# First attention of a vision tower on one Trainium2 core: tokens turned ahead of the last output product, value roots, query sums and the tile table in other places

## The chip, the cores and the metric

The kernel runs on one core of a Trainium2 chip (trn2). The metric is the device time in microseconds (us) of one execution, from inputs in the chip's memory to outputs there. The core's engines are TensorE (PE, matrix products into the PSUM banks; its weight loads are listed as PEld), VectorE (DVE), ScalarE (ACT), GpSimd (POOL) and the queue SP, which only issues transfers here. Each engine works through its own list of instructions in order, and waits on semaphores for the others.

## The reference, cut to what matters

There are 32 samples of 256 tokens with 256 features. Every sample passes a token mixer, then a first attention with 16 heads of 16 key and 64 value features, then a second attention and a layer of 8 experts.

```python
# token mixer
q, k, v = proj(Wq), proj(Wk), proj(Wv)
y = sigmoid(q) * (exp(wb) @ (exp(k) * v)) / (exp(wb) @ exp(k))
h = layer_norm(y @ out_w + out_b + x)           # then a class token is put in front
# first attention, on layer_norm(h)
q, k, v = (l2norm(q), l2norm(k), l2norm(v))
attn = square(relu(einsum('bhid,bhjd->bhij', q, k)))
out = tanh_norm(einsum('bhij,bhjd->bhid', attn, v))
h = h + out @ Wout
# second part: latent attention, then the two best of 8 experts for each token
```

`tanh_norm(t)` is `tanh(n) * t / n` with n the length of t.

## The kernel before, in words

The stages follow each other, each in a block of its own with a barrier of all engines behind it: constants, `mixer_and_attention` (to about 1820 us of the profiled execution), class tokens, `latent_attention` (to about 3029 us), `load_experts`, `plan`, `experts`, `merge`.

`mixer_and_attention` is a software pipeline written out by hand. A loop runs over samples, and in one turn, `sample(i, d, before, more)`, every engine does three things in an order fixed in the code: the products of sample i (eight pairs of heads, p = 0 to 7), the mixer and the projections of the next sample j = i + 1, and the output norm and output product of the sample before, i - 1. Thirty-one turns carry a next sample.

TensorE, for each pair of heads: `sim` (L1105, keys by queries), `attend` (L1115 and L1120, squared weights by values) and `square_sums` (L1127, sums of squares of the outputs, products with only 2 columns). In between stand, for the next sample, the queries and keys of the mixer (`mixer_inputs`, L983 to L989), `mix` (L996), the residual and mixer output, `turn_tokens` (L1031, the transposes of the normed tokens), `project` (L1038), `project_values` (L1062 to L1067), `class_products` (L1075 sums of squares of the keys with 8 columns, L1083, L1087 with 16 columns) and `query_sums` (L1075 again, sums of squares of the queries); and for the sample before `spread_scale` (L1148) and `project_outputs` (L1155, four of them, m = 0 to 3).

What hands over to what, where the change touches it:

- `project_outputs(i-1, 0)` waits for the first scaled outputs OT, which DVE makes (`scale_outputs`, L863). DVE does `first_stats` ahead of it, which in the kernel before ends with two products (L757) that only `first_norm` reads.
- `project_keys` waits for xT, which ACT copies (L613) from the bank that `turn_tokens` fills.
- `attend(i, d, 7)` writes a bank whose sums DVE must have taken (`keep_sums`, L825), and `square_sums(i, 5)` stands directly ahead of it.
- `attend(i, d, 0)` waits for the values V, which POOL scales (`value_rows`, L572). The reciprocal lengths of the values come from a power on POOL (`power`, L66, tile vrn). POOL's order in one turn is: output roots, norm roots, a copy of h1, `class_parts` (L553 to L561), then for each half t of the tokens power, L570 and L572.
- `sim(i, 0)` waits for keys and queries that SP has put through memory (L493 and L502).

`load_experts` loads 16 pieces of expert weights in turns of 4 buffers (SP L2275), splits each into a high part (ACT L2286) and a low part (DVE L2308), makes a few tables on POOL, and at its end writes 16 blocks of zeros into the buffer of routed tokens xg (SP L2279). `plan` then computes on DVE, from the fill of each expert's region, which expert and which row each of 144 tiles has (L2342 to L2369), while SP clears 8 more blocks of xg (L2337).

Of the kernel before, what the change touches and what calls it, by code (L numbers as in the profile page):

```python
# [10 lines left out]
F32 = mybir.dt.float32  # L11
# [360 lines left out]
def mixer_and_attention(nc, v, a, nb):  # L372
# [4 lines left out]
    with ExitStack() as ctx:  # L377
# [158 lines left out]
        @block.gpsimd  # L536
        def _(pool):
            def norm_roots(j):
                pool.wait_ge(ln_stats, 5 * j + 5)
                power(pool, rstd[:, 1], rstd[:, 0], v.inv_root).then_inc(ln_rooted, 1)  # L540
                pool.wait_ge(ln2_stats, 5 * j + 5)
                power(pool, rstd2[:, 1], rstd2[:, 0], v.inv_root).then_inc(ln2_rooted, 1)

            def keep_h1(i, d):
                need(pool, h2_done, i)
                pool.wait_ge(h1_done, LT * i + LT)
                pool.sem_inc(pool_step, 1)
# [17 lines left out]
            def value_rows(j, e, t):  # L565
                pool.wait_ge(v_lift, 2 * j + t + 1)
                power(pool, vrn[:, t], vsm[:, t], v.inv_root).then_inc(v_rn, 1)
                pool.wait_ge(v_rn, 2 * j + t + 1)
                pool.wait_ge(k_inv, j + 1)
                pool.tensor_tensor(vc[:, t], vrn[:, t], rk[:, t], ALU.mult).then_inc(v_c, 1)  # L570
                pool.wait_ge(v_c, 2 * j + t + 1)
                pool.tensor_tensor(V[:, e, t].rearrange("p (g d) -> p g d", d=DV),  # L572
                                   Vr[:, t].rearrange("p (g d) -> p g d", d=DV),
                                   vc[:, t].unsqueeze(2).to_broadcast([P, HEADS, DV]), ALU.mult).then_inc(v_ready, 1)

            def front(j, e):
                norm_roots(j)
                class_parts(j, e)
                value_rows(j, e, 0)
                value_rows(j, e, 1)  # L580
# [130 lines left out]
        def _(dve):  # L711
# [41 lines left out]
            def first_stats(j):  # L753
                dve.wait_ge(hpre_done, j + 1)
                layer_norm_stats(j, mixed, stats, mv, rstd, ln_stats)
                for t in range(LT):
                    dve.scalar_tensor_tensor(ln[:, t], mixed[t], mv[:, t, 0:1], v.g_ln[:], ALU.subtract,  # L757
                                             ALU.mult).then_inc(ln_done, 1)
# [113 lines left out]
            def front(j, e):  # L872
# [5 lines left out]
                first_stats(j)  # L878
                tokens(j + 1)
# [14 lines left out]
            def sample(i, d, before, more):  # L894
# [24 lines left out]
                if before:  # L919
                    scale_outputs(i - 1, 1 - d, 0)  # L920
                    scale_outputs(i - 1, 1 - d, 1)
# [55 lines left out]
        def _(pe):  # L977
            def mixer_inputs(j):
# [5 lines left out]
                last.then_inc(q_done, 1)  # L984
                for t in range(LT):
# [174 lines left out]
            def front(j):  # L1160
                mixer_inputs(j)
# [14 lines left out]
            def sample(i, d, before, more):  # L1176
                j = i + 1
                sim(i, 0)
                if before:
                    square_sums(i - 1, 7)  # L1180
                if more:
                    mixer_inputs(j)
# [23 lines left out]
                square_sums(i, 2)  # L1206
                if before:
# [1045 lines left out]
def load_experts(nc, v, a):  # L2253

    with ExitStack() as ctx:
        NST = 4
# [3 lines left out]
        hi_done, lo_done, idle_clear, misc = sems(nc, ctx, "w_hi", "w_lo", "idle_clear", "d_misc")  # L2260
        block = ctx.enter_context(nc.Block())
        parts = [(v.w1h, v.w1l, e) for e in range(NEXP)] + [(v.w2h, v.w2l, e) for e in range(NEXP)]

        @block.sync
        def _(sp):
# [10 lines left out]
            sp.wait_ge(misc, 6)  # L2276
# [3 lines left out]
            sp.wait_ge(idle_clear, 16 * (v.idle_rows // P))  # L2280

# [7 lines left out]
        def _(pool):  # L2289
            pool.memset(v.zeros[:], 0.0).then_inc(misc, 1)  # L2290
            pool.iota(last_no[:], pattern=[[0, 1]], base=v.out_rows - P, channel_multiplier=1).then_inc(misc, 1)
            for e in range(NEXP):
# [7 lines left out]
                               pattern=[[1, NEXP], [-1, NEXP]], channel_multiplier=0)  # L2300
# [4 lines left out]
        def _(dve):  # L2305
            for n, (h, l, e) in enumerate(parts):
                dve.wait_ge(hi_done, n + 1)
                dve.tensor_tensor(l[:, e], stage[:, n % NST], h[:, e].bitcast(F32), ALU.subtract).then_inc(lo_done, 1)  # L2308


def plan(nc, v):

    with ExitStack() as ctx:
        n_tab = v.tile_no.shape[1]
        n = sbuf(nc, ctx, "p_n", [1, NEXP])
        up = sbuf(nc, ctx, "p_up", [1, NEXP], I32)
        tiles_i = sbuf(nc, ctx, "p_tiles_i", [1, NEXP], I32)
        tiles = sbuf(nc, ctx, "p_tiles", [1, NEXP])
        sums = sbuf(nc, ctx, "p_sums", [1, NEXP, NEXP])
        ends = sbuf(nc, ctx, "p_ends", [1, NEXP])  # L2320
        skip = sbuf(nc, ctx, "p_skip", [1, NEXP])
        tail = sbuf(nc, ctx, "p_tail", [1, NEXP], I32)
        b = sbuf(nc, ctx, "p_b", [1, n_tab])
        past = sbuf(nc, ctx, "p_past", [1, n_tab, NEXP])
        moved = sbuf(nc, ctx, "p_moved", [1, n_tab, NEXP])
        e = sbuf(nc, ctx, "p_e", [1, n_tab])
        row = sbuf(nc, ctx, "p_row", [1, n_tab])
        step, tails, cleared = sems(nc, ctx, "p_step", "p_tails", "p_cleared")
        block = ctx.enter_context(nc.Block())
        fill = v.fill[0:1, v.last_fill]  # L2330

        @block.sync
        def _(sp):
            sp.wait_ge(tails, 1)
            for ex in range(NEXP):
                r = sp.value_load(tail[0:1, ex:ex + 1], min_val=ex * v.rows_e, max_val=(ex + 1) * v.rows_e - P)
                sp.dma_start(v.xg[bass.ds(r, P)], v.zeros[:]).then_inc(cleared, 16)  # L2337
            sp.wait_ge(cleared, 16 * NEXP)

        @block.vector  # L2340
        def _(dve):
            dve.tensor_copy(tail[:], fill).then_inc(tails, 1)  # L2342
            dve.tensor_tensor(n[:], fill, v.region[0:1, :], ALU.subtract).then_inc(step, 1)
            dve.tensor_copy(b[:], v.tile_no[:]).then_inc(step, 1)
            dve.wait_ge(step, 1)
            dve.tensor_scalar(up[:], n[:], float(P - 1), None, ALU.add).then_inc(step, 1)
# [4 lines left out]
            dve.wait_ge(step, 5)  # L2351
            dve.tensor_tensor(sums[:], tiles[:].unsqueeze(1).to_broadcast([1, NEXP, NEXP]), v.upto[0:1],
# [10 lines left out]
            dve.tensor_reduce(e[:], past[:], AX.X, ALU.add).then_inc(step, 1)  # L2363
# [3 lines left out]
            dve.tensor_scalar(v.tile_e[:], e[:], float(NEXP - 1), None, ALU.min).then_inc(step, 1)  # L2367
# [298 lines left out]
def build(nc, a, out):  # L2666
# [14 lines left out]
    with ExitStack() as ctx:  # L2681
# [12 lines left out]
        plan(nc, v)  # L2694
# [73 lines left out]
```

## Time and profile before

| | |
|---|---|
| median of three runs | 3639.7 us (3630.85 to 3646.9) |
| the profiled execution's own time | 3646.67 us |
| its span, first to last instruction | 3643.9 us |
| granted TensorE clock, mean over the span | 0.929 |
| busy share of the span | PE 89%, DVE 58%, ACT 39%, POOL 32% |

The table is read as follows: TensorE is far ahead of the others, and its clock, which has two levels, 2.4 GHz (1.00) and 1.2 GHz (0.50), is at the upper one most of the time. The span leaves 2.8 us of the profiled time outside.

### The profile page before, as it was taken

Reading aid. Unit: us, or ns where it says so; the run is one execution under the profiler, and the core shown is the slowest. Engines: PE = TensorE matmul, PEld = TensorE weight load, DVE = VectorE, ACT = ScalarE, POOL = GpSimd, SP = SyncE. Lnnn points to the kernel's source line nnn. Section 1 sums busy time; section 2 is a strip of 40 time slices with the busy share of each in tenths; the row PEclk is TensorE's granted clock in tenths of the full one; section 3 lists DMA queues with packets and bytes.
Section 4 is the critical chain, followed back from the end, with each engine's and each line's share of the span. In section 5 each row is a group of like instructions: output and inputs, shape, how many; then the busy total and the mean of one; then the engine's idle time right before and its main releaser. Section 6 shows DMA issues by size and latency. Waiting matters only on the chain. (4 is left out here: it accounts for less than half of the span.)

```text
span 3643.9 us, 69402 instructions
## 1 busy us (share of the span) xinstructions
PE 3239.7 (89%) x23216; PEld 2461.1 (68%) x23217; DVE 2117.5 (58%) x5311; ACT 1405.0 (39%) x2820; POOL 1151.8 (32%) x1030
## 2 busy tenths in 40 slices
PE   4899999999999999999977999999999971999990
PEld 2677777777777777777645767777777751999990
DVE  4566656666566666566524666666666653444442
ACT  1443443443443443443412444444444432444440
POOL 2332433423424424424311222222222221444440
PEclk7899999999999999999968999999999995999995
DMA  2232322323323323323300111111111114444449
GB/s 73 76 83 56 78 78 52 86 66 63 86 60 70 86 61 68 86 61 69 81 8 27 34 37 42 44 44 39 36 41 44 41 36 148 77 76 77 76 77 291
DMA packets 219177, 249.00 MB, mean 68 GB/s; under 512 B 36129, under 2 KB 180834, under 8 KB 219122
## 3 DMA queue, kind: packets, MB, share of 16 engines
q1 hardware_dynamic: 184658, 204.82, 21.3%
q0 software_dynamic: 25936, 34.95, 5.8%
q10 hardware_dynamic: 8528, 8.52, 0.7%
q8 instruction: 32, 0.52, 0.1%
q14 instruction: 23, 0.19, 0.0%
HBM read 142.30 MB, written 105.87 MB: 68 GB/s over the span
## 5 line engine op out<-in xcount | busy, mean ns | idle before, releaser
L644 ACT ACTIVATE R<-psA 128x1024 f32<-128x1024 f32 x256 | 262.5, 1025 | 478.3 <-PE psA L1105 476.6
L821 DVE TENSOR_TENSOR PR<-R 128x1024 f32<-128x1024 f32 x256 | 313.6, 1225 | 0.0
L1120 PE MATMUL psA<-PR,V 128*64 128x258 f32 x2048 | 284.1, 398 | 0.0
L1820 DVE TENSOR_REDUCE m_nm<-psC 128x4 f32<-128x516 f32 (+1 forms) x256 | 239.0, 955 | 69.9 <-PE psC L2092 69.3
L1155 PE MATMUL psA<-wout,OT 128*128 128x256 f32 x1024 | 261.5, 400 | 15.5 <-DVE OT L863 15.5
L1691 ACT ACTIVATE m_PT<-psC 128x770 f32<-128x770 f32 x256 | 197.9, 800 | 185.0 <-PE psC L2121 185.0
L1155 PEld LDWEIGHTS psA<-wout,OT 128*128 128x128 f32 x1024 | 188.7, 194 | 48.7 <-DVE OT L863 18.4
L1608 POOL DMA_INDIRECT xg<-r_tn,r_idx x130 | 127.8, 983 | 279.5 <-DMA xg<-r_tn,r_idx 241.2
L1127 PEld LDWEIGHTS psA<-half,osq 128*128 128x128 f32 x1024 | 142.3, 201 | 94.0 <-issue 90.8
L66 POOL TENSOR_TENSOR rstd<-rstd,inv_root 128x2 f32<-128x2 f32 x64 | 45.6, 713 | 469.8 <-DVE rstd L721 469.8
L66 POOL TENSOR_TENSOR vrn<-vsm,inv_root 128x16 f32<-128x16 f32 x64 | 185.2, 2894 | 6.0 <-POOL pcl L561 5.0
L825 DVE COPY ssb<-psA 128x4 f32<-128x4 f32 x256 | 40.6, 159 | 244.9 <-PE psA L1127 243.7
L1120 PEld LDWEIGHTS psA<-PR,V 128*64 128x64 f32 x2048 | 125.8, 138 | 83.4 <-issue 25.9
L66 POOL TENSOR_TENSOR orr<-osm,inv_root 128x32 f32<-128x32 f32 x32 | 174.2, 5443 | 14.7 <-DVE osm L835 14.1
L1680 ACT ACTIVATE m_oa<-psC 128x256 f32<-128x256 f32 x128 | 49.2, 384 | 322.2 <-PE psC L2139 322.2
L649 ACT ACTIVATE oTs<-psA 128x258 f32<-128x258 f32 x256 | 99.0, 387 | 188.8 <-PE psA L1120 184.7
L2422 POOL DMA_INDIRECT out_rows<-e_y,e_dest x69 | 106.8, 1548 | 192.2 <-DVE e_y L2483 189.0
L1127 PE MATMUL psA<-half,osq 128*128 128x2 f32 x1024 | 164.3, 265 | 0.2 <-ACT osq L651 0.2
L2451 ACT ACTIVATE e_sh<-psE 128x512 fp32r<-128x512 f32 x137 | 82.1, 599 | 165.7 <-PE psE L2525 165.7
L2422 POOL DMA_INDIRECT xs<-e_y,e_dest x68 | 105.4, 1550 | 126.4 <-DVE e_y L2483 120.6
L553 POOL TENSOR_TENSOR psq<-prl 80x256 f32<-80x256 f32 x32 | 19.5, 611 | 396.3 <-ACT prl L624 396.3
L1038 PE MATMUL psA<-xT,wqk 128*128 128x256 f32 x512 | 124.8, 399 | 22.0 <-ACT xT L613 22.0
(410 smaller groups left out, 8265.8 us busy)
## 6 DMA issues: line engine op xcount, KB each, us to landing
ks<-parts SPq DMA_DIRECT2D x512, 64.0 KB, 2.2
qs<-parts SPq DMA_DIRECT2D x512, 64.0 KB, 2.3
e_x<-xg SPq DMA_DIRECT2D x143, 129.0 KB
xraw<-in_x SPq DMA_DIRECT2D x66, 256.0 KB
xs<-m_zrow SPq DMA_DIRECT2D x32, 264.0 KB
f_even<-out_rows SPq DMA_DIRECT2D x13, 640.0 KB
f_odd<-xs SPq DMA_DIRECT2D x13, 640.0 KB
out_rows<-f_even ACTq DMA_DIRECT2D x13, 640.0 KB, 5.6
```

Of the source, the lines that this page charges most:

```text
L66: return pool.tensor_tensor(out, x, e.to_broadcast(list(out.shape)), ALU.pow)
L644: act.activation(R[:, p % 2], ps[:, 0:2, :].rearrange("p a (t n) -> p a t n", t=LT), ACT.Relu).then_inc(relu_done, 1)
L649: act.activation(oTs[:, d, p], ps[:, 2 + p % 2, 0:QCOLS], ACT.Copy).then_inc(o_copied, 1)
L821: dve.tensor_tensor(PR[:, p % 2, :, :, 0:L], R[:, p % 2], R[:, p % 2], ALU.mult).then_inc(prob_done, 1)
L1038: last = pe.matmul(ps[:, bank, c * L:(c + 1) * L], v.wqk[:, k, first + c * P:first + (c + 1) * P], xT[:, k, :], start=k == 0, stop=k == KT ...
L1120: last = pe.matmul(ps[64 * hh:64 * hh + 64, 2 + p % 2, 0:QCOLS], V[:, d, t, n * DV:(n + 1) * DV], PR[:, p % 2, hh, t, :], start=False, sto ...
L1127: last = pe.matmul(ps[:, 2 + p % 2, SUMS + 2 * t:SUMS + 2 * t + 2], osq[:, p % 2, t * P:(t + 1) * P], v.half2[:], start=True, stop=True, s ...
L1155: last = pe.matmul(ps[:, BOUT, t * MODEL:(t + 1) * MODEL], OT[:, m % 2, p % 2, t * P:(t + 1) * P], v.wout[:, p, :], start=p == 0 and t == ...
L1608: pool.indirect_dma_start(v.xg, bass.IndirectOffsetOnAxis(ap=idx[rows, d, s, t:t + 1], axis=0), tn[rows, d, s, t], None).then_inc(rows_out ...
L1691: act.activation(PT[:, g % 2, 2 * b:2 * b + 2, :], ps[:, 2 * b:2 * b + 2, 0:3 * P + 1], ACT.Exp).then_inc(exp_done, 1)
L1820: dve.tensor_reduce(nm[:, t, :, DK], ps[:, 0:4, cols], AX.X, ALU.max, negate=True).then_inc(max_done, 1)
L2422: pool.indirect_dma_start(v.odd if b % 2 else out, bass.IndirectOffsetOnAxis(ap=dest[:, b % XD:b % XD + 1], axis=0), y[:, b % XD], None, c ...
```

## The change

On TensorE, within a turn: `mixer_inputs` is cut into `mixer_queries` and `mixer_keys`, and the queries' products stand ahead of `square_sums(i-1, 7)`. `sim(i, 5)` stands ahead of the output products 0 to 2 and the spreads between them. `turn_tokens` stands ahead of output product 3. `query_sums` stands between `square_sums(i, 5)` and `attend(i, d, 7)`, two groups earlier. On DVE: the two products of `first_stats` become `first_scaled` and stand behind `scale_outputs(.., 0)`, and `query_norms` stands ahead of `keep_sums(i, d, 6)`. On POOL: the powers for the values become `value_roots`, and the one for t = 0 stands ahead of `class_parts`. The work of `plan` moves into the block of `load_experts`: on DVE ahead of all low parts, its clears on SP behind the fourth of the 16 weight loads; the wait for the tables is a semaphore instead of the barrier. The block `plan` is gone.

```diff
# POOL
+            def value_roots(j, t):
                 pool.wait_ge(v_lift, 2 * j + t + 1)
                 power(pool, vrn[:, t], vsm[:, t], v.inv_root).then_inc(v_rn, 1)
+
+            def value_rows(j, e, t):
                 pool.wait_ge(v_rn, 2 * j + t + 1)
...
                 keep_h1(i, d)
                 if more:
+                    value_roots(i + 1, 0)
                     class_parts(i + 1, 1 - d)
                     value_rows(i + 1, 1 - d, 0)
+                    value_roots(i + 1, 1)
                     value_rows(i + 1, 1 - d, 1)
# DVE, sample
                     first_stats(j)
                 if before:
                     scale_outputs(i - 1, 1 - d, 0)
+                if more:
+                    first_scaled(j)
+                if before:
                     scale_outputs(i - 1, 1 - d, 1)
...
                     value_lift(j, 1)
+                    query_norms(j, e)
                 keep_sums(i, d, 6)
-                if more:
-                    query_norms(j, e)
# TensorE, sample
                 sim(i, 0)
+                if more:
+                    mixer_queries(j)
                 if before:
                     square_sums(i - 1, 7)
                 if more:
-                    mixer_inputs(j)
+                    mixer_keys(j)
...
                 square_sums(i, 2)
+                sim(i, 5)
                 if before:
                     project_outputs(i - 1, 0)
                     spread_scale(i - 1, 2, more)
                     project_outputs(i - 1, 1)
                     spread_scale(i - 1, 3, more)
                     project_outputs(i - 1, 2)
-                sim(i, 5)
                 attend(i, d, 4)
                 square_sums(i, 3)
+                if more:
+                    turn_tokens(j)
                 if before:
                     project_outputs(i - 1, 3)
                 if more:
-                    turn_tokens(j)
                     project_keys(j)
...
                 square_sums(i, 5)
+                if more:
+                    query_sums(j)
                 attend(i, d, 7)
                 square_sums(i, 6)
-                if more:
-                    query_sums(j)
# load_experts, SP
                 sp.dma_start(dst, src).then_inc(w_loaded[n % NST], 16)
-            sp.wait_ge(misc, 6)
+                if n == NST - 1:
+                    sp.wait_ge(misc, 6)
+                    sp.wait_ge(tails, 1)
+                    for ex in range(NEXP):
+                        r = sp.value_load(tail[0:1, ex:ex + 1], min_val=ex * v.rows_e, max_val=(ex + 1) * v.rows_e - P)
+                        sp.dma_start(v.xg[bass.ds(r, P)], v.zeros[:]).then_inc(cleared, 16)
...
             sp.wait_ge(idle_clear, 16 * (v.idle_rows // P))
+            sp.wait_ge(cleared, 16 * NEXP)
# load_experts, DVE: the instructions of plan (L2342 to L2369), then
+            for n, (h, l, e) in enumerate(parts):
+                dve.wait_ge(hi_done, n + 1)
+                dve.tensor_tensor(l[:, e], stage[:, n % NST], h[:, e].bitcast(F32), ALU.subtract).then_inc(lo_done, 1)
# build
         load_experts(nc, v, a)
-        plan(nc, v)
         experts(nc, v, out)
```

## Rows read from the trace of the kernel before

**Rows 1.** The page, section 1: busy us, share of the span, instructions.

```profile
PE 3239.7 (89%) x23216; PEld 2461.1 (68%) x23217; DVE 2117.5 (58%) x5311; ACT 1405.0 (39%) x2820; POOL 1151.8 (32%) x1030
```

**Rows 2.** Waits of PE, 150 to 1800 us: line, releaser, us in total, times, longest.

```profile
PE psA L1038 <- ACT xT L613: 20.6, 30, 0.7
PE psA L1155 <- DVE OT L863: 15.1, 30, 0.5
PE psA L1115 <- DVE ssb L825: 9.8, 30, 0.3
PE psA L1115 <- POOL V L572: 3.5, 3, 1.2
```

**Rows 3.** Timeline of PE, starts of project_keys: start us, us, line, [idle before <-releaser].

```profile
524.58 2.64 PE L1038 MATMUL psA<-xT,wqk 128*128 128x256 f32 x11 [0.69 <-ACT xT L613]
...
581.68 1.56 PE L1038 MATMUL psA<-xT,wqk 128*128 128x256 f32 x6 [0.69 <-ACT xT L613]
...
1244.30 1.99 PE L1038 MATMUL psA<-xT,wqk 128*128 128x256 f32 x8 [0.69 <-ACT xT L613]
...
1297.73 1.56 PE L1038 MATMUL psA<-xT,wqk 128*128 128x256 f32 x6 [0.69 <-ACT xT L613]
...
1739.63 2.64 PE L1038 MATMUL psA<-xT,wqk 128*128 128x256 f32 x11 [0.69 <-ACT xT L613]
```

**Rows 4.** Timeline of PE, 1038 to 1048 us: class products, end of a turn.

```profile
1038.13 0.96 PE L1087 MATMUL psA<-wqc,xT 128*128 128x16 f32 x8
...
1043.98 0.38 PE L1115 MATMUL psA<-pcl,vcls 80*128 80x258 f32 x1 [0.33 <-DVE ssb L825]
...
1045.32 0.61 PE L1127 MATMUL psA<-half,osq 128*128 128x2 f32 x4
1045.78 1.04 PE L1075 MATMUL psA<-ind,qsq 128*128 128x8 f32 x8
1046.75 0.50 PE L1105 MATMUL psA<-qs,ks 64*128 64x256 f32 x4
1047.18 0.61 PE L1127 MATMUL psA<-half,osq 128*128 128x2 f32 x4
1047.65 1.60 PE L983 MATMUL psA<-x,wq_bd 128*128 128x256 f32 x4
```

**Rows 5.** Windows: us, busy PE PEld DVE ACT POOL (instructions), clock, DMA share, GB/s.

```profile
150.00:1816.00 1666.00, 1615.26 (x8992) 1190.18 (x8990) 1046.55 (x2319) 694.54 (x1329) 596.37 (x428) 0.95 0.30 72
...
983.00:984.00 1.00, 1.00 (x7) 1.00 (x7) 1.00 (x1) 0.16 (x1) 0.00 (x0) 0.64 0.51 137
...
1044.70:1048.10 3.40, 3.40 (x30) 2.76 (x27) 1.25 (x5) 1.38 (x3) 3.24 (x4) 1.00 0.78 201
...
1048.00:1049.00 1.00, 1.00 (x4) 0.63 (x3) 0.39 (x2) 0.40 (x1) 1.00 (x1) 0.57 1.16 176
```

**Rows 6.** Timeline of DVE and PE, 1020 to 1026 us: normed tokens, their transposes.

```profile
1020.68 0.73 DVE L773 TENSOR_SCALAR xn<-h,mv,rstd 128x256 f32<-128x256 f32 x2
...
1025.84 0.60 PE L1031 MATMUL psA<-ident,xn 128*128 128x128 f32 x4
```

**Rows 7.** Timeline of DVE, POOL and PE, 1255 to 1270 us, the values' chain.

```profile
1255.16 0.17 DVE L806 TENSOR_SCALAR vsm<-vss 128x16 f32<-128x16 f32 x1
...
1256.84 0.61 POOL L553 TENSOR_TENSOR psq<-prl 80x256 f32<-80x256 f32 x1 [12.04 <-ACT prl L624]
...
1267.56 1.90 POOL L572 TENSOR_TENSOR V<-Vr,vc 128x1024 f32<-128x1024 f32 x1
...
1269.70 0.35 PE L1115 MATMUL psA<-pcl,vcls 80*128 80x258 f32 x1 [1.17 <-POOL V L572]
```

**Rows 8.** Timeline, 3069 to 3082 us: plan, then the experts' first loads.

```profile
3069.44 0.16 DVE L2342 CAST p_tail<-fill 1x8 int32<-1x8 f32 x1 [6.85 <-PEq L52]
...
3070.63 8.00 SPq L2337 DMA_DIRECT2D xg<-zeros  x8
...
3081.91 31.73 SPq L2400 DMA_DIRECT2D e_x<-xg  x13
```

More of the change, by code:

```diff
@@ L577, in front @@
                 norm_roots(j)
+                value_roots(j, 0)
                 class_parts(j, e)
                 value_rows(j, e, 0)
+                value_roots(j, 1)
                 value_rows(j, e, 1)
@@ L755, in first_stats, with first_scaled @@
                 layer_norm_stats(j, mixed, stats, mv, rstd, ln_stats)
+            def first_scaled(j):
                 for t in range(LT):
@@ L920, in sample @@
                     scale_outputs(i - 1, 1 - d, 0)
+                if more:
+                    first_scaled(j)
+                if before:
                     scale_outputs(i - 1, 1 - d, 1)
@@ L977, in _, with mixer_queries @@
         def _(pe):
-            def mixer_inputs(j):
+            def mixer_queries(j):
                 pe.wait_ge(x2_ready, j + 1)
@@ L984, in mixer_inputs, with mixer_keys @@
                 last.then_inc(q_done, 1)
+            def mixer_keys(j):
                 for t in range(LT):
@@ L1178, in sample @@
                 sim(i, 0)
+                if more:
+                    mixer_queries(j)
                 if before:
@@ L1181, in sample @@
                 if more:
-                    mixer_inputs(j)
+                    mixer_keys(j)
                 sim(i, 1)
@@ L2255, in load_experts @@
     with ExitStack() as ctx:
+        n_tab = v.tile_no.shape[1]
+        rows = sbuf(nc, ctx, "p_n", [1, NEXP])
+        up = sbuf(nc, ctx, "p_up", [1, NEXP], I32)
+        tiles_i = sbuf(nc, ctx, "p_tiles_i", [1, NEXP], I32)
+        tiles = sbuf(nc, ctx, "p_tiles", [1, NEXP])
+        sums = sbuf(nc, ctx, "p_sums", [1, NEXP, NEXP])
+        ends = sbuf(nc, ctx, "p_ends", [1, NEXP])
+        skip = sbuf(nc, ctx, "p_skip", [1, NEXP])
+        tail = sbuf(nc, ctx, "p_tail", [1, NEXP], I32)
+        b = sbuf(nc, ctx, "p_b", [1, n_tab])
+        past = sbuf(nc, ctx, "p_past", [1, n_tab, NEXP])
+        moved = sbuf(nc, ctx, "p_moved", [1, n_tab, NEXP])
+        expert = sbuf(nc, ctx, "p_e", [1, n_tab])
+        row = sbuf(nc, ctx, "p_row", [1, n_tab])
         NST = 4
@@ L2260, in load_experts @@
         hi_done, lo_done, idle_clear, misc = sems(nc, ctx, "w_hi", "w_lo", "idle_clear", "d_misc")
+        step, tails, cleared = sems(nc, ctx, "p_step", "p_tails", "p_cleared")
         block = ctx.enter_context(nc.Block())
         parts = [(v.w1h, v.w1l, e) for e in range(NEXP)] + [(v.w2h, v.w2l, e) for e in range(NEXP)]
+        fill = v.fill[0:1, v.last_fill]
         @block.sync
@@ L2299, in _ @@
             pool.affine_select(out=v.upto[:], in_=v.upto[:], compare_op=ALU.is_ge, fill=0.0, base=0,
-                               pattern=[[1, NEXP], [-1, NEXP]], channel_multiplier=0)
+                               pattern=[[1, NEXP], [-1, NEXP]], channel_multiplier=0).then_inc(misc, 1)
             pool.affine_select(out=v.identd[:], in_=v.identd[:], compare_op=ALU.not_equal, fill=1.0, base=0,
@@ L2305, in _ @@
         def _(dve):
[L2306 to L2341, printed above, removed]
             dve.tensor_copy(tail[:], fill).then_inc(tails, 1)
-            dve.tensor_tensor(n[:], fill, v.region[0:1, :], ALU.subtract).then_inc(step, 1)
+            dve.wait_ge(misc, 6)
+            dve.tensor_tensor(rows[:], fill, v.region[0:1, :], ALU.subtract).then_inc(step, 1)
             dve.tensor_copy(b[:], v.tile_no[:]).then_inc(step, 1)
             dve.wait_ge(step, 1)
-            dve.tensor_scalar(up[:], n[:], float(P - 1), None, ALU.add).then_inc(step, 1)
+            dve.tensor_scalar(up[:], rows[:], float(P - 1), None, ALU.add).then_inc(step, 1)
             dve.wait_ge(step, 3)
@@ L2351, in _ @@
             dve.wait_ge(step, 5)
+            dve.wait_ge(misc, 7)
             dve.tensor_tensor(sums[:], tiles[:].unsqueeze(1).to_broadcast([1, NEXP, NEXP]), v.upto[0:1],
@@ L2362, in _ @@
                               ALU.mult).then_inc(step, 1)
-            dve.tensor_reduce(e[:], past[:], AX.X, ALU.add).then_inc(step, 1)
+            dve.tensor_reduce(expert[:], past[:], AX.X, ALU.add).then_inc(step, 1)
             dve.wait_ge(step, 10)
@@ L2366, in _ @@
             dve.wait_ge(step, 11)
-            dve.tensor_scalar(v.tile_e[:], e[:], float(NEXP - 1), None, ALU.min).then_inc(step, 1)
+            dve.tensor_scalar(v.tile_e[:], expert[:], float(NEXP - 1), None, ALU.min).then_inc(step, 1)
             dve.wait_ge(step, 12)
             dve.scalar_tensor_tensor(v.tile_row[:], b[:], float(P), row[:], ALU.mult, ALU.add).then_inc(step, 1)
+            for n, (h, l, e) in enumerate(parts):
+                dve.wait_ge(hi_done, n + 1)
+                dve.tensor_tensor(l[:, e], stage[:, n % NST], h[:, e].bitcast(F32), ALU.subtract).then_inc(lo_done, 1)
 def experts(nc, v, out):
```

1 line of the change is left out of this document (removed).

## The prediction

> **What bounds the kernel now.** I read the page's busy shares first: TensorE works 3239.7 of 3643.9 us, no other engine over 58% [rows 1]. In the first attention, 150 to 1816 us, it is nearer still to full: 1615.26 of 1666 us [rows 5]. In this stage, then, time can come only from TensorE's own waits, from its clock, or from fewer products, and the change has the same products. The waits view names the waits, each about once a turn: 20.6 us before `project_keys` for xT, 15.1 before the first output product for OT, 9.8 before `attend(7)` for the sums, together 45.5 us in 30 turns, 1.52 a turn. Values from POOL are rarer, 3 times [rows 2].
>
> The starts of `project_keys` in the timeline then show that turns differ [rows 3]: 57.10 us from 524.58 to 581.68, 53.43 us from 1244.30 to 1297.73, and on average (1739.63 - 524.58) / 22 = 55.23 us. The windows view tells why: in some stretches TensorE is busy throughout while its clock is at 0.50, the 1.2 GHz level. In windows of 1 us I find 35 such stretches between 150 and 1816 us, each 3.4 or 6.8 us long; one row stands for each of two kinds [rows 5]. Eight of the 35 begin behind the class products, as the one at 983, all 3.4 us long. The other 27 begin at the end of the turn, as the one at 1048, 9 of 3.4 us and 18 of 6.8. In pieces of 3.4 that is 8 + 9 + 36 = 53, or 180 us of low clock; at half speed 90 us are lost, 3.0 a turn, 1.7 a piece. A check: the long turn has three pieces, so 57.10 - 5.1 = 52.0; the short one has none but waits 1.17 us for V [rows 7], so 52.3. A turn at full clock takes 52.0, and 55.2 is that, 3.0 for the clock and some waits for V.
>
> What stood ahead of the fall at 1048? From 1045.32 to 1047.65 (2.33 us) there are two `square_sums` (2 columns, 0.46 us to the next start), the 8 products of `query_sums` (8 columns, 0.97), and one `sim` of 0.43 as the only wide work [rows 4]: 1.90 us narrow. TensorE was busy for all of the 3.40 us ahead of the fall, at clock 1.00 [rows 5]. Here the clock falls after narrow products, without a gap.
>
> **The change part by part.** *Output product 0.* `sim(5)` (0.43 us, as `sim` in [rows 4]) runs in the wait for OT, and DVE makes OT before the two L757 products, not behind them. The 15.1 us go. `sim(5)` itself waits for the ReLU of pair 4, whose `sim` lies two spreads, an `attend` and a `square_sums` earlier; behind a late ReLU all of TensorE would queue, but those last over 2 us, by the 1.34 of `attend` and the 0.46 of `square_sums` [rows 4]. L757 now delays only `first_norm`, and TensorE has no wait in that chain [rows 2].
>
> *Turned tokens.* An output product, 8 products of 256 columns, or 1.9 us by the 11 that take 2.64 [rows 3], takes the place of the wait of 0.69, so the 20.6 us go. The normed tokens are due those 1.9 us and the 0.7 of the other edits sooner; they were ready at 1021.4, 4.4 us before the transposes [rows 6]. ACT's copies of xT come earlier too. DVE's `result`, and SP's store of it, come about 1 us later against the keys; SP's next work waits for the low parts of the queries, behind two projections, so nothing there moves.
>
> *Query sums.* They lie in the wait for `keep_sums(5)`, and the 9.8 us go. DVE takes them (`query_norms`) before `keep_sums(6)`, which is not due until the `square_sums` behind `attend(7)`, 1.34 us on. `mixer_queries`, now ahead of `square_sums(7)`, waits for `query_norms`: it stands 1.34 + 0.46 + 0.43 = 2.2 us behind the sums [rows 4]. I cost that at nothing, with a bound of 0.3 a turn. The three waits make 45.5.
>
> *The clock.* The turn's end becomes `square_sums` and `query_sums` (1.4 us narrow), `attend(7)` (1.34 wide), `square_sums` (0.46), `sim` (0.43 wide), the queries' products (4 of 256 columns, 0.96 wide), `square_sums` (0.46). The densest 3.3 us now hold 1.9 narrow in two lumps with 1.3 wide between. The class products are the nearest case in the trace: a `square_sums`, a `sim`, 8 products of 8 columns, 4 of 256, 8 of 16 [rows 4] make 2.3 narrow in 3.6, and the clock fell behind them in 8 of 30 turns, to one piece each. The new end is milder, so 0 to 8 falls there. Behind the class products, which are untouched, falls may become more frequent, as the turns change their length: 8 to 16. That gives 8 to 24 pieces, or 32 if those at the end still last 6.8 us. I take 20, nearer to the case that it resembles: 68 us low, 34 lost instead of 90, a gain of 56. The outer bounds are 0 (53 pieces remain) and 90 (none).
>
> The Trainium skill, page "TensorE: Matmul & The Clock Gate", section "Why this matters for your kernels", lays a fall of the clock to idle gaps between bursts of matmuls. The busy stretch ahead of the fall at 1048 disagrees with gaps as the only cause; by the page the reordering would give nothing here, and the sum would be 56 us smaller.
>
> *Chain of the values.* In the turn without a fall `attend(0)` came 1269.70 - 1244.30 = 25.40 after the keys, 1.17 of it a wait for V [rows 3, 7]; without the 0.33 for the sums TensorE would be there at 23.90. POOL's chain of V, in the order class part, power, product, power, product, ran from 1256.84 to 1269.46, 12.6 us. It now starts with the power, which needs the lifted sums of 1255.33 and not the ReLU [rows 7]. The same 12.6 us then end at 23.7, plus about 0.1 to start. So V comes just in time: 0 to 0.2 us a turn, in turns without a fall. I charge 2 us. Had the power stayed where it was, the wait would be 1.5. The class part comes later by the power, but is first used in the next turn.
>
> *Queries from memory.* `sim(0)` comes 0.33 earlier; what its transfers have to spare is in no row. 0 to 0.33 a turn, 0 to 10 us; I take 1, since no wait for them is among the larger ones [rows 2].
>
> *Tile table.* From the first operation of `plan` to the first load of the experts lie 3081.91 - 3069.44 = 12.5 us [rows 8], with TensorE idle; they go. In exchange the low parts and SP's weight loads 5 to 16 wait for the table and for 8 clears of 8.00 us together [rows 8]. The delay is between 0 and 8.0; I take 3.5, since load 5 had to wait for the first low part before as well. All later weights, the idle blocks and the barrier ahead of the experts hang on it. Gain 9, bounds 4 and 12.
>
> *Sum*, against the profiled execution's 3646.7: 45.5 + 56 - 2 - 1 + 9 = 107.5, so 3539. That execution lay 7.0 above the median of the runs; on that scale, 3532.
>
> **The rivals.** *A, the clock does not follow:* the low pieces stay at 53, because falls hang on gaps or on something not seen. 45.5 + 9 - 3 = 51.5 gained, 3588. For it: all narrow products are still there. Against it: falls come where these are densest. The skill's rule above is this case. *B, another chain ends each turn:* V or the queries come 1 us late in every turn once TensorE is faster. 30 us are given back, 3562. For it: the slack that I find is 0 to 0.2 us. *C, slower:* the query sums now stand one `attend` behind the last value products, closer to the fall of the class products. If falls there last 6.8 us, and those at the end come in every turn with 6.8, the pieces are 4 a turn, 120 in place of 53: 67 x 1.7 = 114 lost, 3639.7 - 51.5 + 114 = 3702. It decides from 53 + 51.5 / 1.7 = 83 pieces, 2.8 a turn. Against it: no turn in the trace had more than three. *D, the change doesn't do what it says:* each hidden wait returns at the next handover (OT of product 1, the sums of pair 6) and the clock stays. Only the table's 9 us remain, 3631.
>
> **How the numbers follow.** The forecast 0.70, A 0.13, B 0.07, C 0.05, D 0.05. The forecast's own bounds: 90 + 45.5 + 12 gained, 3492; with 32 pieces 36 + 45.5 + 4 - 16, 3570. The range 3500 to 3592 takes in A and B. What a measurement of this kernel can tell from no change is about 0.5%, 18 us. Faster by more: forecast, A and B, 0.90. Within: D, 0.05. Slower: C, 0.05.
>
> **What would show it.** In TensorE's waits view the rows for xT, OT and the sums are gone, and that for V stays under 5 us. Turns without a fall last 50.5 to 50.7 us. Low stretches at the turn's end are under 10, and the mean clock from 150 to 1816 us rises from 0.95 to 0.98. After the last low part the experts' loads follow with no `plan` between, and the weight loads pause behind the fourth. The forecast is wrong if turns without a fall stay at 52, if V or the queries appear as releaser in most turns, or if the low stretches only move.

## The result, and the profile after

The changed kernel takes 3533.2 us (median of four runs, 3517.6 to 3538.7) against 3635.3 (3630.4 to 3646.9): a ratio of 0.971, 95% interval 0.967 to 0.975. The forecast was 3532. The profiled execution has a span of 3533.4 us against 3643.9, 110.5 less, where the sum had 107.5; its terms were further off than that, and in both directions. Medians and ratios in this document are of undisturbed executions alone; three of the study, of 4649 to 6145 us, are left out.

Waits of TensorE in the same 30 turns, line, releaser, us in total, times, longest; they answer to [rows 2]:

```profile
PE psA L1128 <- POOL V L574: 28.6, 23, 1.4
PE psA L994 <- DVE qm L818: 3.2, 14, 0.2
PE psA L1118 <- DMA qs<-parts: 0.7, 2, 0.4
PE psA L1051 <- ACT xT L619: 0.7, 1, 0.7
```

The rows for OT and for the sums are gone, that for xT has its first turn left. In their place stands the wait for V, in 23 of 30 turns and eight times as large in total as before.

The windows view over the stage, and inside one fall of the clock (columns as in [rows 5]):

```profile
150.00:1690.00 1540.00, 1505.84 (x8870) 1125.89 (x8869) 1041.68 (x2297) 681.84 (x1305) 613.95 (x420) 0.99 0.32 76
...
776.00:777.00 1.00, 0.86 (x4) 0.76 (x3) 0.41 (x3) 0.83 (x1) 0.97 (x1) 0.62 1.11 270
777.00:778.00 1.00, 1.00 (x4) 0.72 (x4) 0.60 (x2) 0.19 (x1) 1.00 (x1) 0.50 1.00 189
```

In windows of 1 us there are now 7 falls in 30 turns, all at the turn's end, 12 pieces of 3.4 us in place of 53. None is left behind the class products.

A turn without a fall, in TensorE's timeline:

```profile
1011.48 0.47 PE L1128 MATMUL psA<-pcl,vcls 80*128 80x258 f32 x1
1011.87 1.09 PE L1133 MATMUL psA<-PR,V 128*64 128x258 f32 x8
1012.90 0.61 PE L1140 MATMUL psA<-half,osq 128*128 128x2 f32 x4
1013.36 0.63 PE L1044 MATMUL psA<-ident,xn 128*128 128x128 f32 x4
1013.83 1.89 PE L1168 MATMUL psA<-wout,OT 128*128 128x256 f32 x8
1015.56 3.62 PE L1051 MATMUL psA<-xT,wqk 128*128 128x256 f32 x16
...
1031.40 0.61 PE L1140 MATMUL psA<-half,osq 128*128 128x2 f32 x4
1031.87 1.04 PE L1088 MATMUL psA<-ind,qsq 128*128 128x8 f32 x8
1032.76 0.36 PE L1128 MATMUL psA<-pcl,vcls 80*128 80x258 f32 x1
...
1035.35 1.10 PE L994 MATMUL psA<-x,wq_bd 128*128 128x256 f32 x4 [0.23 <-DVE qm L818]
...
1040.76 0.36 PE L1128 MATMUL psA<-pcl,vcls 80*128 80x258 f32 x1 [1.35 <-POOL V L574]
```

The transposes hand over to the output product after 0.47 us, and the keys follow it without a wait. The next keys begin at 1067.12, so the turn lasts 51.56 us; without the 1.35 for V it would be 50.2. Over the 23 turns without a fall the mean is 51.40. The mean of 30 turns is 51.84, against 55.34.

The values' chain on POOL in the same turn, and VectorE beside it, which answer to [rows 7]:

```profile
1026.61 3.99 POOL L66 TENSOR_TENSOR vrn<-vsm,inv_root 128x16 f32<-128x16 f32 x1 [8.99 <-DVE vsm L814]
1030.57 0.61 POOL L553 TENSOR_TENSOR psq<-prl 80x256 f32<-80x256 f32 x1
...
1033.18 1.90 POOL L574 TENSOR_TENSOR V<-Vr,vc 128x1024 f32<-128x1024 f32 x1
1035.19 2.89 POOL L66 TENSOR_TENSOR vrn<-vsm,inv_root 128x16 f32<-128x16 f32 x1
...
1038.46 1.90 POOL L574 TENSOR_TENSOR V<-Vr,vc 128x1024 f32<-128x1024 f32 x1
```

```profile
1026.63 1.22 DVE L829 TENSOR_TENSOR PR<-R 128x1024 f32<-128x1024 f32 x1
...
1033.46 1.66 DVE L814 TENSOR_SCALAR vsm<-vss 128x16 f32<-128x16 f32 x1
1035.03 0.18 DVE L818 TENSOR_SCALAR qm<-psA 128x32 f32<-128x32 f32 x1
```

The first power takes 3.99 us and not 2.89, and so it is, within 0.1 us, in 29 of 31 turns. It starts together with VectorE's square of pair 7, which takes 1.22. And `vsm`, 0.17 us in [rows 7], takes 1.66 here: it ends when POOL's product of 1033.18 ends.

The weights and the table, which answer to [rows 8]; SP issues, the weights' high and low parts and the first load of the experts:

```profile
2923.43 1.93 SPq L2309 DMA_DIRECT2D w_stage<-in_w  x4
...
2926.44 8.12 SPq L2315 DMA_DIRECT2D xg<-zeros  x8
...
2931.60 0.29 DVE L2375 SCALAR_TENSOR_TENSOR tile_row<-p_b,p_row 1x144 int32<-1x144 f32 x1
2931.82 4.61 DVE L2378 TENSOR_TENSOR w1l<-w_stage,w1h 128x1024 fp32r<-128x1024 f32 x4
...
2934.61 19.38 SPq L2309 DMA_DIRECT2D w_stage<-in_w  x12
...
2954.03 8.61 SPq L2318 DMA_DIRECT2D xg<-zeros  x16
...
2969.75 11.47 SPq L2409 DMA_DIRECT2D e_x<-xg  x7
```

The table is ready at 2931.9, but the fifth weight load waits until 2934.6 for the clears. From the first weight load to the first load of the experts it is 46.3 us; in the kernel before it was 52.0 (from 3029.95 to 3081.91).

### The profile page after: what moved, and what is told of

Same layout as the page of the kernel before. It is cut to its first block and busy times, and to the rows that moved or that the text cites. A ratio compares the mean times of both kernels' runs of the same rounds, so it can differ in the third digit from the quotient of the medians.

```text
span 3533.4 us, 69391 instructions
## 1 busy us (share of the span) xinstructions
PE 3149.0 (89%) x23216; PEld 2412.9 (68%) x23217; DVE 2118.9 (60%) x5311; ACT 1404.8 (40%) x2820; POOL 1181.1 (33%) x1030
## 5 line engine op out<-in xcount | busy, mean ns | idle before, releaser
L66 POOL TENSOR_TENSOR vrn<-vsm,inv_root 128x16 f32<-128x16 f32 x64 | 216.8, 3388 | 304.5 <-DVE vsm L814 301.1
L1140 PE MATMUL psA<-half,osq 128*128 128x2 f32 x1024 | 156.1, 257 | 0.0
L2484 DVE TENSOR_TENSOR e_sl<-psE,e_sh 128x512 fp32r<-128x512 f32 x137 | 94.8, 692 | 75.3 <-ACT e_sh L2460 75.3
L1118 PE MATMUL psA<-qs,ks 64*128 64x256 f32 x1024 | 130.3, 333 | 7.8 <-DMA qs<-parts 7.2
```

What stands on the lines that cost most here:

```text
L66: return pool.tensor_tensor(out, x, e.to_broadcast(list(out.shape)), ALU.pow)
L1118: last = pe.matmul(ps[:, hh, t * L:(t + 1) * L], ks[rows, p, t * P:(t + 1) * P], qs[rows, p, :], start=True, stop=True, skip_group_check=True)
L1140: last = pe.matmul(ps[:, 2 + p % 2, SUMS + 2 * t:SUMS + 2 * t + 2], osq[:, p % 2, t * P:(t + 1) * P], v.half2[:], start=True, stop=True, s ...
```

## The experiments

"Pieces" are, as in the prediction, low stretches of the clock counted in 3.4 us, over the 30 turns of the profiled execution. The experiments ran at four times (1 to 4, 5 to 8, 9 and 10, 11), and the kernel before, run beside each group, took 3632 to 3642 us; a difference of less than 10 us between groups is therefore shown by the mean turn and the ratio, not by the medians. Pieces are those of one execution: the two kernels with the attention of before, the kernel before and the seventh, have 53 and 59. All eleven:

| kernel | us | ratio to before (95%) | mean turn | pieces: class products, turn's end, behind V | wait for V |
|---|---|---|---|---|---|
| before | 3635.3 | | 55.34 | 8, 45, 0 | 3.5 |
| changed | 3533.2 | 0.971 (0.967 to 0.975) | 51.84 | 0, 12, 0 | 28.6 |
| 1 root behind | 3552.2 | 0.976 (0.972 to 0.980) | 52.61 | 0, 4, 10 | 53.1 |
| 2 sums at end | 3551.5 | 0.976 (0.972 to 0.980) | 52.29 | 0, 22, 0 | 17.4 |
| 3 mix ahead | 3519.1 | 0.967 (0.963 to 0.971) | 51.27 | 12, 12, 0 | 0 |
| 4 lift behind | 3538.7 | 0.973 (0.968 to 0.978) | 51.94 | 0, 13, 0 | 29.4 |
| 5 sums alone | 3628.5 | 0.998 (0.996 to 1.000) | 54.85 | 13, 20, 7 | 26.3 |
| 6 waits alone | 3569.4 | 0.984 (0.982 to 0.986) | 53.08 | 0, 46, 0 | 0 |
| 7 table alone | 3625.9 | 0.999 (0.998 to 1.001) | 55.62 | 11, 48, 0 | 2.3 |
| 8 class apart | 3504.5 | 0.965 (0.964 to 0.967) | 50.95 | 0, 15, 0 | 0 |
| 9 apart, sums at end | 3532.9 | 0.971 (0.967 to 0.975) | 51.66 | 0, 23, 0 | 0 |
| 10 sums halved | 3495.5 | 0.959 (0.955 to 0.963) | 50.61 | 0, 8, 0 | 0 |
| 11 queries behind | 3568.0 | 0.980 (0.976 to 0.984) | 53.07 | 0, 46, 0 | 0 |

**1. The power for the values back behind the class part.**

```diff
                 if more:
-                    value_roots(i + 1, 0)
                     class_parts(i + 1, 1 - d)
+                    value_roots(i + 1, 0)
                     value_rows(i + 1, 1 - d, 0)
```

> The changed kernel with only POOL's part undone: the power for the values of t = 0 stands behind the class part again. In the changed kernel V comes late in 24 turns (33.0 us in all), and the power for t = 0 takes 3.99 us where it took 2.89. Theory one (the power, moved ahead, now meets a product of VectorE and loses 1.1 us, so the move was worth little): the power takes 2.89 again, V's chain ends 0.3 to 0.4 us later against the keys, the wait for V is about 1.65 us in turns without a fall, the time is 8 to 12 us more than the changed kernel's 3533, about 3542. Theory two (the move was worth the 1.5 us a turn that the forecast gave it): the wait grows to 2.8 us, 36 us more, about 3569.

Measured: 19 us more than the changed kernel. All powers for the values take 2.89 us again, and `attend(0)` starts 25.53 us after the keys instead of 25.20, so theory one holds for the chain: the move was worth 0.33 us. The time is more than it allowed, for a reason neither theory had. The wait is now 1.74 to 1.97 us in most turns, and behind it the clock falls in 10 of 30 turns. Timeline and windows of one:

```profile
1056.34 0.36 PE L1128 MATMUL psA<-pcl,vcls 80*128 80x258 f32 x1 [1.97 <-POOL V L574]
1056.62 1.09 PE L1133 MATMUL psA<-PR,V 128*64 128x258 f32 x8
1057.64 3.64 PE L1009 MATMUL psA<-ewT,ekv 128*128 128x256 f32 x8
```

```profile
1056.00:1057.00 1.00, 0.67 (x5) 0.49 (x7) 1.00 (x1) 0.00 (x0) 1.00 (x1) 1.00 1.18 145
1057.00:1058.00 1.00, 1.00 (x9) 0.54 (x6) 0.11 (x1) 0.24 (x1) 1.00 (x1) 0.80 1.16 142
1058.00:1059.00 1.00, 1.00 (x3) 0.81 (x3) 0.00 (x0) 0.42 (x2) 1.00 (x1) 0.50 0.39 45
```

`mix` (L1009) takes 3.64 us here and 1.99 in a turn without a fall. So gaps do count; they are not all. The Trainium skill, page "TensorE: Matmul & The Clock Gate", section "Why this matters for your kernels", also has the clock fall behind idle gaps, though longer ones than these. In the changed kernel waits for V of 0.93 to 1.35 us are followed by a fall in none of 23 turns.

**2. The query sums back at the end.**

```diff
                 square_sums(i, 5)
-                if more:
-                    query_sums(j)
                 attend(i, d, 7)
                 square_sums(i, 6)
+                if more:
+                    query_sums(j)
# and query_norms(j, e) back behind keep_sums(i, d, 6)
```

> The changed kernel with only the query sums (TensorE) and query norms (VectorE) back behind square_sums(6) and keep_sums(6); the mixer's queries stay ahead of square_sums(7). Theory N (narrow products in one lump make the clock fall): the low stretches at the turn's end come back, from 12 pieces of 3.4 us to 25 or more, 22 us or more lost on the clock, and about 0.33 to 0.46 us a turn for the sums of pair 5, together 3562 to 3590. Theory G (the clock fell for gaps or for something else): the pieces stay near 12, and only the wait comes back, 10 to 14 us, about 3545.

Measured: 18 us more, 22 pieces at the turn's end for 12. The direction is that of theory N, the number between the two. The wait for V went from 28.6 to 17.4 us: TensorE, slowed at the turn's end, arrives later at V. Part of what the clock takes there is thus time in which it would have waited, and the time of this kernel cannot price a piece.

**3. The wait for V filled.**

```diff
                 sim(i, 1)
-                attend(i, d, 0)
                 if more:
                     mix_keys(j)
+                attend(i, d, 0)
                 sim(i, 2)
```

> The changed kernel with one more exchange on TensorE: mix_keys stands ahead of attend(0), in the time in which TensorE waits for V. If the wait for V is all that ends the turn there, the 33 us of that wait go to under 5, turns without a fall last 50.2 us instead of 51.5, and with the clock's pieces at 12 the time is 3503. The rival: mix_keys itself waits for the exponentials of the keys (up to 0.7 us a turn is then given back, 3520), or turns of another length meet more falls (each piece 1.7 us, up to 20 more of them, 3535).

Measured: 3519.1, 14 us less than the changed kernel (17 by the mean turns). The wait for V is gone altogether, and `mix_keys` waits for nothing. Of its 28.6 us half was given back: 12 falls behind the class products came back, none of which the changed kernel has. The second rival was right on the mechanism.

**4. The power after the square instead of beside it.**

```diff
                     value_sums(j, 1)
-                    value_lift(j, 0)
                 prob(i, d, 7)
                 if more:
+                    value_lift(j, 0)
                     key_norms(j)
```

> The changed kernel with VectorE's lifted sums of t = 0 put behind the square of pair 7 (L829) instead of ahead of it, so that POOL's power starts when that product has ended. Theory one (the 1.1 us that the power lost were spent blocked by that product, which reads two operands from SBUF): the power starts 1.3 us later, takes 2.89 us, and V comes 0 to 0.3 us later than in the changed kernel, time 3533 to 3541. Theory two (the power is long because it is the first work after 9 us of idleness on POOL, or for another reason of its own): it takes 3.99 still, V comes 1.3 us later, and 30 us are added, about 3565.

Measured: 3538.7, and every power for the values between 2.89 and 2.90 us (the view of the tile vrn; minimum, median, maximum in ns):

```profile
L66 POOL TENSOR_TENSOR vrn<-vsm,inv_root x64: 2893/2893/2900, 92.9 to 1711.3; 128x16 f32<-128x16 f32 x64
```

In the changed kernel the same line reads (29 of the 64 took 3.90 us or more):

```profile
L66 POOL TENSOR_TENSOR vrn<-vsm,inv_root x64: 2893/2896/3990, 92.6 to 1707.4; 128x16 f32<-128x16 f32 x64
```

POOL was idle 10 us ahead of the power here too, so theory two falls: the 1.1 us were lost where the power and the square start together. V comes as in the changed kernel, `attend(0)` starting up to 25.18 us after the keys.

**5, 6, 7. Parts of the change alone, in the kernel before.** The fifth has the query sums, query norms and mixer's queries of the diff above, the sixth `sim(5)`, `first_scaled` and `turn_tokens`, the seventh `load_experts` with the table, without `plan`.

> The kernel before with one part of the change alone: query sums ahead of attend(7), query norms ahead of keep_sums(6), the mixer's queries ahead of square_sums(7). Theory N (a lump of narrow products makes the clock fall): of 53 low pieces of 3.4 us at most 25 remain, 48 us or more come back on the clock, and 0.46 us a turn, 14 us, for the wait that is covered; in the turns that no longer fall TensorE comes 1.5 us before V, which takes 25 to 40 us back. Together 3635 less 62 plus 33, about 3605, with the wait for V as the largest row. Theory G (falls come from gaps, or from something else): 45 or more pieces remain, only the 14 us come, about 3621, and V waits stay rare.

Measured: a gain of 4 us (15 by the mean turns). The pieces go from 53 to 40, less far than N said; 13 of them lie behind the class products and 7 behind waits for V of 1.74 to 1.94 us. 26.3 us of wait for V, 23 more than before, take back most of what the clock and the covered wait give. The part that the forecast gave 56 + 10 us is worth 4 to 15 by itself.

> The kernel before with another part alone: sim(5) ahead of output product 0, L757 behind scale_outputs(0), tokens turned ahead of output product 3. The waits for OT and xT go. If what they cost is the idle time that the waits view shows (0.50 and 0.69 us), a turn at full clock becomes 1.2 us shorter, 36 us in all. If it is the distance between the starts of the neighbouring products (1.12 against 0.54 us, and 1.29 against 0.47), it becomes 1.4 us shorter, 42 us. The low pieces stay between 45 and 60, all with the same lump at the turn's end; then the time is 3593 to 3599. The rival: the lump at the end is met in every turn or in few, as the turns have another length, and the clock adds or takes 20 us.

Measured: 3569.4, a gain of 63 us, over 20 more than expected. The pieces are 46, 7 fewer, which makes 12. The turn at full clock is 53.08 - 46 x 1.7 / 30 = 50.5, against 52.2: 1.7 us shorter, and not 1.2 or 1.4. The rest is read in the timelines: output product 2 lasts 1.92 us to the next start before, with a `sim` behind it (1019.88 to 1021.80), and 1.65 after, with an `attend` behind it (1009.83 to 1011.48).

> The kernel before with the tile table alone made beside the expert weights and the block plan gone. The forecast gave it 9 us, 3626. In the profile of the changed kernel the stretch from the first weight load to the first load of the experts is 46.3 us, against 52.0 before, since the weight loads 5 to 16 begin 5 us later: by that the gain is 5.6 us, 3630. The attention is untouched, about 53 low pieces and the waits of before.

Measured: 3625.9 against 3632.2; the interval of the ratio takes in 1, so the time shows no difference. The profile is clearer: 47.1 us from the first weight load to the experts' first load, 4.8 less than before.

The three gains add up to 73 us, and the whole change brings 102. None of the three has POOL's move. Experiment 1 is the three parts together without it: 83 us below its kernel before, 10 more than their sum, which is within what such sums leave open. POOL's move, on top of the three, makes the other 19. It was not run alone.

**8. Class products in two lumps.** On top of the third:

```diff
                 if more:
-                    class_products(j)
+                    key_sums(j)            # the first line of class_products
                     project_values(j, 2)
+                    class_products(j)      # the rest
                     project_values(j, 3)
```

> The changed kernel with mix_keys ahead of attend(0) (the third experiment, 3519 us, 24 low pieces, 12 of them behind the class products) and one more edit: the key sums (8 products of 8 columns) stay behind sim(7), but value product 2 (1.4 us wide) stands between them and the other class products. Theory N: the narrow work there falls in two lumps of 1.5 and 0.8 us, and the falls behind the class products go from 12 to 0 to 3, while those at the end may change; 12 to 20 us less, about 3502. Rival: the falls there stay (G), or as many come back at the turn's end as go here, 3519; or POOL's class part, 1.4 us later, delays V again, which the waits view would show.

Measured: 3504.5, 15 us less by the medians and 10 by the mean turns. The 12 falls behind the class products are gone, and the pieces at the turn's end go from 12 to 15. POOL's later class part delays nothing.

**9. The second experiment without a wait for V.** On top of the eighth, the edit of the second.

> The eighth experiment (no wait for V, class products in two lumps, 15 low pieces, all at the turn's end, 3504.5 us) with only the query sums and query norms back behind square_sums(6) and keep_sums(6). This is the second experiment without the wait for V, which there covered part of what the clock lost. Theory N (the lump decides): low pieces at the turn's end go from 15 to 35 or more, 34 us or more, and 14 us for the wait for the sums of pair 5: 3552 or more. Theory G (gaps decide): the pieces stay near 15, and the time is 3519.

Measured: 3532.9, 28 us more by the medians, of which the kernels before beside them, 3632.2 and 3641.9, explain a part. The profiles say 21 us in 30 turns (51.66 against 50.95). The pieces go from 15 to 23, not to 35, and the turns without a fall last 50.33 us instead of 50.04, since the wait for the sums is back and the one for the query norms is gone: 8 x 1.7 and 30 x 0.29 make 22, so the price of 1.7 us a piece holds once nothing covers it. Theory N expected too many falls, and 23 is nearer to theory G's 15; what the lump does is decided by the eleventh.

**10. The query sums in two halves.** On top of the eighth:

```diff
                     project_values(j, 3)
+                    query_sums_first(j)    # 4 products, tokens 0 to 127
                 attend(i, d, 6)
                 square_sums(i, 5)
                 if more:
                     query_sums(j)          # 4 products, tokens 128 to 255
                 attend(i, d, 7)
```

> The eighth experiment with the query sums in two halves: the four products of the first 128 tokens stand ahead of attend(6), the other four stay between square_sums(5) and attend(7). The lump at the turn's end shrinks from 1.44 to about 0.95 us narrow, and the one ahead of attend(6) is 0.5 us. Theory N: the pieces at the turn's end go from 15 to under 8, 12 us or more, 3492. The rival: about half of the wait for the sums of pair 5 comes back (0.1 us a turn at most), and the falls stay near 15 or move elsewhere, 3504 to 3508.

Measured: 3495.5 and 8 pieces, counted in an execution of 3505.1; by the mean turns 10 us less than the eighth. This is the fastest kernel of the study, 0.959 of the kernel before (0.955 to 0.963) and 38 us below the changed one.

**11. The mixer's queries back.** On top of the ninth:

```diff
                 sim(i, 0)
-                if more:
-                    mixer_queries(j)
                 if before:
                     square_sums(i - 1, 7)
                 if more:
+                    mixer_queries(j)
                     mixer_keys(j)
```

> The ninth experiment with the mixer's queries (0.96 us wide) back behind square_sums(7), so that the turn's end on TensorE is again that of the kernel before: square_sums, query_sums, sim, square_sums without the wide work between. Theory N: the low pieces at the turn's end go from 23 to 40 to 50, as the kernel before has 45; 29 to 46 us more than 3533, about 3570. The rival (the query sums' place was all that mattered there, and what lay in the kernel before beyond 23 pieces came from its other length of turn): 20 to 28 pieces, 3528 to 3542.

Measured: 3568.0, and 46 pieces at the end of the turn, a fall in each of 30 turns; the kernel before has 45 there, in 27 turns. Against the ninth only the place of the mixer's queries differs. Both have the same wait of 0.3 us, and a turn at full clock, the mean less 1.7 a piece, is of the same length (50.4 and 50.5 us), so neither the gap nor the length of the turn explains the 23 more pieces. TensorE's waits in this kernel, all of them:

```profile
PE psA L1131 <- DVE ssb L833: 9.8, 30, 0.3
PE psA L1121 <- DMA qs<-parts: 1.1, 1, 1.1
```

The windows view from 150 to 1650 us of the eighth and the eleventh:

```profile
150.00:1650.00 1500.00, 1494.32 (x8799) 1119.32 (x8799) 1032.24 (x2268) 672.19 (x1300) 614.99 (x417) 0.98 0.34 78
```

```profile
150.00:1650.00 1500.00, 1488.16 (x8434) 1106.43 (x8433) 1012.95 (x2176) 645.49 (x1246) 594.05 (x402) 0.95 0.32 75
```

TensorE is busy for over 99% of both. The eleventh's only regular gap is 0.3 us, and its clock is at 0.95. Busy is the profile's own reckoning, in which the ends of matrix products are modelled: idle time inside a run of narrow products would not show.

## Why the prediction was right, and where it was not

*The forecast's own sign of being wrong came.* It named three: turns without a fall that stay at 52, V as releaser in most turns, low stretches that only move. V is the releaser in 23 of 30 turns, and turns without a fall last 51.4 us, where 50.5 to 50.7 was given. The 28.6 us of wait are rival B, nearly at its price of 30. That the time came out at the forecast is luck: two gains were larger than forecast by about as much as this loss.

*Covered waits: right place, too small.* The three rows went as the forecast said. Their worth was taken from the idle time of the waits view, 45.5 us. A turn at full clock without a wait for V became 52.2 - 50.2 = 2.0 us shorter, 60 us in 30 turns. The idle time in a row starts when the last product before it is reckoned to end; the distance between starts is what a cover saves. Read so, in the turns at full clock, the move of `sim(5)` saves 0.85 us a turn (0.57 for the wait, and 0.27 because the output product ahead of its old place is shorter), that of the transposes 0.90 (1.29 us to the start of the keys became 0.47 to the next product, and output product 3 is 0.08 shorter), that of the query sums 0.48, and the query norms take 0.23 back: 2.0.

*The clock: right mechanism, too small.* 12 pieces and not 20, so 41 x 1.7 = 70 us and not 56. At the turn's end the comparison with the class products held: 7 falls, where 0 to 8 were given. Behind the class products 8 to 16 were given and none came. What the changed kernel's lack of falls there hangs on was not settled. The third experiment, with the same products but turns of another length, has 12. They go when that lump is parted, in the eighth. Rival C's 120 pieces and rival D's unchanged clock did not come.

*The rule of the Trainium skill* that was rival A ("TensorE: Matmul & The Clock Gate", "Why this matters for your kernels") would have left the 53 pieces. Experiments 8, 9 and 11 decide against gaps that the profile shows as the only cause: 15, 23 and 46 pieces with hardly a gap. Experiment 1 shows that a gap of 1.74 to 1.97 us among busy work can be enough too.

*Chain of the values: wrong.* "The same 12.6 us then end at 23.7" failed. TensorE was there at 1039.41, 23.85 after the keys (23.90 was said), but V only let it start at 25.20. The chain took 13.75 us, since the first power lost 1.10 beside VectorE's square. Another 0.3 went between V's end and the start of `attend`. The charge of 2 us was 28.6. The Trainium skill, page "SBUF — State Buffer", section "SBUF: two separate sides", has a rule for it: VectorE and GpSimd share a pair of ports, and whichever instruction starts first holds it to its end while the other waits, VectorE's with two operands from SBUF among them. The trace agrees in part: the power loses 1.10 beside a square of 1.22, it loses nothing when it starts behind it (experiment 4), and `vsm` waits 1.5 us for POOL's product and ends with it. By the records the power that lost had started 0.02 first, so which of the two holds the ports is not read from them. The trace differs for powers that are already running: a square starts inside each of the 31 later powers for the values and inside 31 powers for the output roots (orr), and neither side takes longer than alone.

```profile
1040.32 5.42 POOL L66 TENSOR_TENSOR orr<-osm,inv_root 128x32 f32<-128x32 f32 x1
...
1040.59 1.22 DVE L829 TENSOR_TENSOR PR<-R 128x1024 f32<-128x1024 f32 x1
```

In experiment 1 the powers for the output roots start within 0.02 us of a square in 28 turns, and take 6.47 us instead of 5.41:

```profile
L66 POOL TENSOR_TENSOR orr<-osm,inv_root x32: 5413/6467/6469, 163.5 to 1774.2; 128x32 f32<-128x32 f32 x32
```

What counts for a power is thus a square that starts at the same time. The prediction moved a POOL instruction without asking what VectorE does at that time.

*Query norms: inside the bound, but not nothing.* They were costed at nothing, with a bound of 0.3 a turn. The waits view shows 14 waits of 0.23, 3.2 us; by the starts, the mixer's queries begin 0.66 us behind `sim(0)` on average where 0.43 is the distance without a wait, 7 us in all. The norms are late because `vsm` ahead of them is blocked: in experiment 1 no `vsm` takes over 0.2 us, and there is no such wait.

*Tile table: too large.* 5.6 us and not 9. The delay of the fifth weight load was 5 us and not 3.5; the 8 clears on SP made it, not the table on VectorE. Alone it cannot be told from nothing in the time.

*The sum.* 60 + 70 - 25 + 5.6 = 111, against 110.5 measured, where 25 is the wait for V less the 3.5 of before. The first two come from the mean turns with the pieces and waits taken off, so the sum closes by itself; the distances between starts above are the check on it. The forecast's 107.5 was near because the gains from covered waits and clock were taken 28 us too small, the loss to V 23 us too small and the table's gain 3 us too large. Of the parts run alone, the query part brought 4 to 15 us where the forecast's terms for it were 66, and the waits part 63 where they were 36: a term read from the kernel before does not say what it is worth by itself.

## What to carry to other kernels

When TensorE is the bound, look at its granted clock in windows of 1 us, and mix products of few columns with wide ones: the same instructions in another order (experiments 8 and 11) moved 31 pieces of low clock, 53 of the 63 us between them. When waits are covered, ask what comes last next: here 1.1 us of a 1.5 us move on POOL were lost beside a VectorE square, and an exchange of two groups on TensorE (experiment 3) removed the new wait. Price a covered wait by the distance between starts, not by the idle time shown.

## What the runs showed of the hardware that was not expected

- TensorE's clock falls to the 1.2 GHz level with the engine busy by the profile and no regular gap above 0.33 us, when products of 2 to 16 columns stand close together (46 pieces in experiment 11). It also falls behind waits of 1.74 to 1.97 us (10 turns of experiment 1), not behind waits of 0.93 to 1.35 us (23 turns of the changed kernel).
- A GpSimd power of 2.89 us took 3.90 to 3.99 in 29 of the 31 turns in which it started within 0.1 us of a VectorE product of two SBUF tiles (1.22 us), and one of 5.41 took 6.47; with the same product started 0.26 us or more behind the power, neither lost anything (62 cases in the changed kernel). A VectorE operation of 0.17 us took 1.66 during a GpSimd product.
- An output product, 8 products of 256 columns on 128 rows, takes 1.92 us to the next start when a product on 64 rows (`sim`) or 48 rows (the spreads) follows, 1.65 when `attend` with its 80 rows follows, and 1.73 when the keys with 128 rows follow. Why was not tried.
